# A gated delta-rule layer on one core: z's gates a body later, the heads' sum on ScalarE and GpSimd, weights in three pieces, new engine orders

## The reference

```python
mixed = hidden_states @ w_qkv
z = (hidden_states @ w_z).reshape(Bq, Sq, NUM_V_HEADS, DV)
b, a = hidden_states @ w_b, hidden_states @ w_a
mixed = jax.nn.silu(_causal_conv(mixed, conv_w))          # 4 taps
q, k, v = jnp.split(mixed, [KEY_DIM, 2 * KEY_DIM], axis=-1)
beta = jax.nn.sigmoid(b)
g = -jnp.exp(A_log) * jax.nn.softplus(a + dt_bias)
def step(state, xs):                                      # q, k l2-normalised
    state = state * jnp.exp(g_t)[..., None, None]
    kv = jnp.einsum('bhk,bhkv->bhv', k_t, state)
    delta = (v_t - kv) * b_t[..., None]
    state = state + jnp.einsum('bhk,bhv->bhkv', k_t, delta)
    return state, jnp.einsum('bhk,bhkv->bhv', q_t, state)
o = outs * jax.nn.silu(z)
o = o * jax.lax.rsqrt(jnp.mean(o * o, axis=-1, keepdims=True) + EPS) * norm_gamma
return o.reshape(Bq, Sq, VALUE_DIM) @ w_out               # the sum over the heads
```

## Time and profile before

| | us |
|---|---|
| median of 3 runs | 2320.44 |
| lowest, highest | 2314.27, 2321.96 |
| profiled execution | 2318.31 |
| its span, first to last instruction | 2316.6 |

### The profile page before, as it was taken

How to read it: one execution, slowest core, us unless ns; L and a number is a source line. 1 busy time by engine, 2 the same in 40 slices (tenths; PEclk the granted TensorE clock), 3 DMA queues, 4 the chain that set the end, 5 groups by cost and what they waited for, 6 DMA issues and landing times. The chain is left out here.

```text
span 2316.6 us, 47612 instructions
## 1 busy us (share of the span) xinstructions
PE 2153.8 (93%) x16494; PEld 1561.7 (67%) x16494; DVE 1843.2 (80%) x3303; ACT 1198.6 (52%) x3805; POOL 1224.3 (53%) x1194
## 2 busy tenths in 40 slices
PE   6899999999999999999999999999999999977998
PEld 3667677666777676767777676767676776754665
DVE  4788788888888888888888887888888788853665
ACT  3555555555655555655555565555565555531110
POOL 3555566565666565566655565655566565530100
PEclk8999999999999999999999999999999999989999
DMA  4587777788777778777777777878878878761000
GB/s 138 130 174 165 181 157 165 158 167 183 165 164 167 162 169 183 171 169 162 166 163 169 183 166 163 161 164 172 183 164 161 157 155 172 156 166 37 28 10 19
DMA packets 597341, 349.81 MB, mean 151 GB/s; under 512 B 487664, under 2 KB 558704, under 8 KB 596848
## 3 DMA queue, kind: packets, MB, share of 16 engines
q1 hardware_dynamic: 597104, 346.78, 68.9%
HBM read 159.50 MB, written 69.73 MB: 99 GB/s over the span
## 5 line engine op out<-in xcount | busy, mean ns | idle before, releaser
L1343 DVE SCALAR_TENSOR_TENSOR conv<-bank,cw_all,conv 128x511 f32<-128x511 f32 (+2 forms) x768 | 568.1, 740 | 18.3 <-ACT conv L1235 6.9
L1056 PE MATMUL bank<-xT,w_kh 128*128 128x512 f32 x1024 | 559.6, 630 | 10.6 <-ACT kraw L1264 10.1
L1288 ACT ACTIVATE X<-bank 128x512 f16<-128x512 f32 x384 | 229.8, 598 | 286.0 <-PE bank L1109 285.9
L1369 DVE TENSOR_TENSOR N<-bank,lev 128x512 f16<-128x512 f32 x320 | 218.5, 683 | 151.1 <-PE bank L1099 151.0
L1235 ACT ACTIVATE conv<-bank,cw_all 128x512 f32<-128x512 f32 x256 | 175.9, 687 | 289.5 <-PE bank L1056 289.5
L1184 PE MATMUL bank<-ogT,wo 128*128 128x512 f32 x512 | 268.3, 628 | 24.4 <-DMA ogT<-o_blocks 23.9
L985 POOL TENSOR_SCALAR_AFFINE_SELECT mhiT<-m32T 128x512 f16<-128x512 f32 x128 | 131.2, 1025 | 255.6 <-DVE m32T L1355 255.6
L1075 PE MATMUL bank<-w_kh,xT 128*128 128x256 f32 x1024 | 248.9, 386 | 0.4 <-DVE conv L1343 0.4
L1075 PEld LDWEIGHTS bank<-w_kh,xT 128*128 128x128 f32 x1024 | 189.8, 192 | 54.0 <-DVE conv L1343 23.7
L1099 PEld LDWEIGHTS bank<-X,mhiT 128*128 128x128 f16 x3072 | 139.9, 98 | 122.4 <-issue 110.5
L1387 DVE SCALAR_TENSOR_TENSOR rhs<-bank,sc_all,vals 128x128 f32<-128x128 f32 x384 | 116.0, 344 | 108.2 <-PE bank L1136 108.2
(11 more groups left out here) (178 smaller groups left out, 4851.9 us busy)
## 6 DMA issues: line engine op xcount, KB each, us to landing
egb<-rows SPq DMA_DIRECT2D x64, 512.0 KB, 4.9
v_blocks<-conv SPq DMA_DIRECT2D x64, 512.0 KB, 3.4
ecb<-rows SPq DMA_DIRECT2D x64, 512.0 KB, 5.2
vT<-v_blocks SPq DMA_DIRECT2D x256, 128.0 KB, 3.2
o_blocks<-og SPq DMA_DIRECT2D x64, 512.0 KB, 3.7
ogT<-o_blocks SPq DMA_DIRECT2D x256, 128.0 KB, 4.3
w_kh<-w_heads SPq DMA_DIRECT2D x16, 768.0 KB, 7.4
XT<-X SPq DMA_TRANSPOSE x384, 3.6
```

Of the source, the lines that this page charges most:

```text
L1056: mm = pe.matmul(PB[j % 2][:, :], w[:, k, g * P:(g + 1) * P], xT[:, k, b * SEQ:(b + 1) * SEQ], start=(k == 0), stop=(k == KT - 1))
L1288: act.activation(blocks(X[:, p], i, 0), packed(IB[p], i), ACT.Copy).then_inc(s_x[p], 1)
L1343: dve.scalar_tensor_tensor(conv[:, g, m:], PB[j % 2][:, 0:SEQ - m], cw_all[:, head, g * TAPS + 3 - m:g * TAPS + 4 - m], conv[:, g, m:], op ...
L1369: dve.tensor_tensor(N[:, p].rearrange("p x (b s) -> p x b s", s=LEVELS[i]), packed(IB[p], i), blocks(lev[:, 1 + i:2 + i, :], i, 0).broadca ...
```

## The change

**z's gates.** `gate` 0 and 1 are done for body k+2 in round k, and `gate` 2 and 3 for body k+1 in the next round's beginning (before: all for body k+3). The banks P0 and P1 therefore hold z of another body than before when `proj` comes, and the waits follow:

```diff
-                        if j < 2 and later:
-                            pe.wait_ge(s_zs, 2 * (n - 1) + j + 1)
+                        if j < 2 and n == 1:
+                            pe.wait_ge(s_conv, 3 * (2 + j) + 3)
+                        if j < 2 and n > 1:
+                            pe.wait_ge(s_zs, 2 * (n - 2) + j + 1)
...
                     if c == 0:
-                        pe.wait_ge(s_conv, 12 * n + 3 * (2 + h) + 3)
+                        pe.wait_ge(s_conv, 12 * min(n + 1, BODIES - 1) + 3 * (2 + h) + 3)
+                        if n == BODIES - 1:
+                            pe.wait_ge(s_zs, 2 * (n - 1) + h + 1)
```

```diff
-                elif name == "acc":
-                    dve.wait_ge(s_opp, n * 2 + i + 1)
...
-                    dve.tensor_tensor(a, OB[i][:, :], a, ALU.add).then_inc(s_acc, 1)
...
+                elif name == "ev":
+                    act.wait_ge(s_opp, n * 2 + i + 1)
+                    act.activation(flat(og2)[:, SEQ * i:SEQ * (i + 1)], OB[i][:, :], ACT.Copy).then_inc(s_ev, 1)
...
+                elif name == "add":
+                    b = n % B
+                    pool.wait_ge(s_ev, 2 * n + i + 1)
...
+                    pool.tensor_tensor(a, flat(og2)[:, SEQ * i:SEQ * (i + 1)], a, ALU.add).then_inc(s_acc, 1)
...
                     if c % 2 == 0 and later:
-                        pe.wait_ge(s_acc, 2 * (n - 1) + c // 2 + 1)
+                        pe.wait_ge(s_ev, 2 * (n - 1) + c // 2 + 1)
...
-                        act.wait_ge(s_ost[1 - n % 2], 16 * ((n - 1) // 2 + 1))
+                        act.wait_ge(s_acc, 2 * n)
```

```diff
-            def weights(kh):
-                if kh > 1:
+            def weights(kh, j):
+                third = slice(256 * j, 256 * (j + 1))
+                if j == 0 and kh > 1:
                     sp.wait_ge(s_proj, 4 * B * (kh - 1))
                     sp.wait_ge(s_zp, 2 * B * (kh - 1))
-                sp.dma_start(w_kh[:, kh % 2], w_heads[kh].rearrange("p (t n) -> p t n", t=KT)).then_inc(s_w, 16)
-                if kh > 0:
-                    sp.wait_ge(s_wog, kh)
-                sp.dma_start(wo_raw[:, :, :], w_out[kh]).then_inc(s_wo, 16)
+                sp.dma_start(w_kh[:, kh % 2, :, third],
+                             w_heads[kh].rearrange("p (t n) -> p t n", t=KT)[:, :, third]).then_inc(s_w, 16)
+                if j == 2:
+                    if kh > 0:
+                        sp.wait_ge(s_wog, kh)
+                    sp.dma_start(wo_raw[:, :, :], w_out[kh]).then_inc(s_wo, 16)
...
-                    if n % B == 1 and n // B + 1 < KH:
-                        weights(n // B + 1)
+                    if n % B > 0 and n // B + 1 < KH:
+                        weights(n // B + 1, n % B - 1)
```

**The orders.** All five lists of `ORDER` are new. SP's:

```diff
-        ("ecs", 0, 2), ("weights", 0, 4), ("flip", 1, 2), ("vld", 0, 2), ("ost", 0, 0), ("flip", 2, 2), ("egs", 0, 4),
-        ("old", 0, 0), ("flip", 3, 2), ("flip", 4, 2), ("x0", 0, 3), ("flip", 5, 2), ("flip", 0, 3), ("vst", 0, 3),
+        ("flip", 5, 1), ("flip", 1, 2), ("weights", 0, 3), ("egs", 0, 3), ("ost", 0, 0), ("vst", 0, 2), ("ecs", 0, 4),
+        ("flip", 2, 2), ("old", 0, 0), ("vld", 0, 2), ("flip", 3, 2), ("x0", 0, 3), ("flip", 4, 2), ("flip", 0, 3),
```

More of the change, by code:

```diff
@@ L31 @@
     "tensor": [
[L32 to L40, removed]
+        ("proj", 0, 3), ("newton", 0, 1), ("join", 1, 2), ("newton", 1, 1), ("proj", 1, 3), ("gate", 2, 1),
@@ new lines @@
+        ("gate", 3, 1), ("growx", 1, 2), ("finish", 0, 1), ("finish", 1, 1), ("proj", 2, 3), ("join", 2, 2),
+        ("solve", 0, 1), ("proj", 3, 3), ("write", 0, 1), ("ktp", 0, 3), ("ktp", 1, 3), ("products", 1, 2),
+        ("read", 1, 1), ("growx", 2, 2), ("products", 0, 3), ("solve", 1, 1), ("proj", 4, 3), ("write", 1, 1),
+        ("ktp", 2, 3), ("ktp", 3, 3), ("join", 3, 2), ("proj", 5, 3), ("read", 2, 1), ("growx", 3, 2), ("proj", 6, 3),
+        ("solve", 2, 1), ("proj", 7, 3), ("write", 2, 1), ("join", 4, 2), ("project", 0, 0), ("project", 1, 0),
@@ L41 @@
+        ("project", 2, 0), ("project", 3, 0), ("growx", 4, 2), ("read", 3, 1), ("out", 0, 1), ("out", 1, 1),
+        ("gate", 0, 2), ("gate", 1, 2), ("solve", 3, 1), ("join", 0, 3), ("join", 5, 2), ("out", 2, 1),
+        ("growx", 0, 3), ("growx", 5, 2), ("out", 3, 1),
     ],
     "scalar": [
-        ("zs", 1, 1), ("tap", 0, 2), ("growx", 1, 1), ("u", 0, 0), ("tap", 1, 2), ("silu", 0, 2), ("squares", 0, 2),
-        ("kraw", 0, 2), ("growx", 2, 1), ("u", 1, 0), ("silu", 1, 2), ("tap", 2, 2), ("squares", 1, 2), ("u", 2, 0),
@@ L45 @@
-        ("growx", 3, 1), ("tap", 3, 2), ("growx", 4, 1), ("vals", 0, 1), ("vals", 1, 1), ("silu", 2, 2),
-        ("join", 5, 1), ("u", 3, 0), ("silu", 3, 2), ("growx", 5, 1), ("growx", 0, 2), ("power", 0, 0), ("zs", 0, 2),
-        ("power", 1, 0),
+        ("power", 1, 0), ("tap", 0, 3), ("zs", 1, 1), ("growx", 1, 2), ("u", 0, 1), ("silu", 0, 3), ("tap", 1, 3),
+        ("squares", 0, 3), ("kraw", 0, 3), ("growx", 2, 2), ("u", 1, 1), ("silu", 1, 3), ("squares", 1, 3),
+        ("growx", 3, 2), ("u", 2, 1), ("tap", 2, 3), ("ev", 0, 0), ("tap", 3, 3), ("vals", 0, 2), ("vals", 1, 2),
@@ L48 @@
+        ("growx", 4, 2), ("ev", 1, 0), ("silu", 2, 3), ("silu", 3, 3), ("zs", 0, 2), ("join", 5, 2), ("u", 3, 1),
+        ("growx", 0, 3), ("growx", 5, 2), ("power", 0, 1),
     ],
     "vector": [
-        ("join", 1, 2), ("tt", 0, 1), ("tt", 1, 1), ("conv", 0, 3), ("conv", 1, 3), ("conv", 2, 3), ("s", 0, 1),
-        ("join", 2, 2), ("conv", 3, 3), ("rhs", 1, 1), ("ot", 0, 0), ("conv", 4, 3), ("conv", 5, 3), ("p", 0, 2),
-        ("s", 1, 1), ("p", 1, 2), ("join", 3, 2), ("rhs", 2, 1), ("conv", 6, 3), ("conv", 7, 3), ("scan", 0, 3),
@@ L233, in build_kernel @@
         s_opp = sem("s_opp")
+        s_ev = sem("s_ev")
         s_acc = sem("s_acc")
@@ L1215, in _ @@
             for name, i, n in rounds(ORDER["tensor"]):
+                if name == "gate" and n == BODIES - 1:
+                    continue
                 run(name, i, n)
+                if (name, i, n) == ("gate", 3, BODIES - 2):
+                    for j in range(4):
+                        run(name, j, BODIES - 1)
                 if n == 0 and (name, i) == ("proj", 2):
@@ L1318, in _ @@
             for name, i, n in rounds(ORDER["scalar"]):
+                if name == "zs" and n == BODIES - 1:
+                    continue
                 run(name, i, n)
+                if (name, i, n) == ("zs", 1, BODIES - 2):
+                    for j in range(2):
+                        run(name, j, BODIES - 1)
                 if n == 0 and (name, i) == ("tap", 0):
```

25 lines of the change are left out of this document (14 added, 11 removed).

## The result

The changed kernel takes 2484.15 us (median of 4 runs, 2482.26 to 2489.66) against 2319.10 for the kernel before (4 runs): a ratio of 1.0718, with the 95% interval 1.0692 to 1.0744. It is 7% slower, and it lies 59 us above the upper end of the range. The profiled execution took 2489.7 us, its span 2487.9.

A forecast was written before the change was run, and what follows sets the result against it. PE was taken to bound the kernel, so only its waits and clock count. From 2318.3 us: - 107 + 78 + 51 + 20 + 6 + 1 = + 49, that is 2367 us; 8-in-10 range 2240 to 2425.

The forecast's parts named there:

- The sign: Whole kernel: slower by over 0.3%, chance 0.60; within 0.3%, 0.05; faster, 0.35.
- B: Rival at growx3: the DMA backlog drains in time, no wait there; 2218 to 2258 us, chance 0.26.
- C: Rival at growx3: backlog drains in part, 0.2 to 0.8 us wait per body; 2255 to 2317 us, chance 0.13.
- D: Rival at ACT's queue: growx4 1 us late delays flip4 and growx5, 60 us more; about 2427 us, chance 0.07.
- What bounds it: Whole kernel: PE, busy 93% of the span, sets the time; edits count only through its idle time or clock.
- (a): Weights in three later pieces: SP no longer stands before wo_raw, saving 3.34 us x 14 = 47 us.
- (b): New order, PE's small waits for S, kraw, XT and project go: together 60 us saved.
- (c): SP's new order: four loads ahead of flip2 make growx3 wait, 78 us; weights' pieces add 51 us.
- The clock: At the third weights piece, a 3.0 us stall lowers PE's clock: 1.3 us x 15 = 20, bounds 0 and 60.
- (e): Heads' sum from DVE to ACT and POOL: costed at nothing, but about 1 us at the last body's end.
- (d): z's gates a body later: proj 2 waits for ACT's silu, at most 0.1 us a body, 6 in all.

The follow-up runs named there:

- the good one: The SP order of the kernel with ecb behind flip3 (2199.48 us); the same kernel with w_kh in one 768 KB transfer took 2232.53 us.
- ecb behind flip3: Changed kernel with SP's list alone rearranged: v_blocks and egb issued ahead of flip1, ecb behind flip3; 2199.48 us, ratio 0.9473 to the kernel before.
- egb, ecb by ACT: Changed kernel with egb and ecb issued by ACT behind its growx1, ecb for body k+3 instead of k+4; 2303.77 us, ratio 0.9930 to the kernel before.
- only egb ahead: Changed kernel with egb issued ahead of flip1, leaving three 512 KB transfers between the flips; 2388.30 us, ratio 1.0275 to the kernel before.
- spread: Changed kernel with SP's list alone rearranged: v_blocks and egb ahead of flip1, ecb behind flip2; 2379.92 us, ratio 1.0253 to the kernel before.
- the old order, with pieces: Kernel before with w_kh alone changed, to three pieces at the same place of SP's list; 2294.70 us, ratio 0.9868 to the kernel before.
- The new order with the sum on DVE: Kernel with ecb behind flip3, but the heads' sum put back on DVE; 2233.46 us, ratio 0.9634 to the kernel before.

## Why the prediction was wrong

The sign and the mechanism of the loss were right: the queue of four 512 KB transfers between flip1 and flip2 makes growx3 wait in nearly every body (61 waits). Of the other cases B (the backlog drains) and C (in part) fell with the 196 us of waits; the ceiling of 435 GB/s that stands beside B was nowhere near, as the row moved 259. D (ACT's queue) fell too: 196 of the 206.5 us for XT stand before growx3, so growx5 can have 10.5 at most, where D needs 60. Step by step:

- **What bounds it.** Right. PE's idle time and clock account for the differences above, but for the sum's in the new order, which hides in PE's busy time.
- **(a) The weights, -47.** Right in kind, and in size -31.6 in the old order and -33 in the good one. This step took the whole loss away, and left out that the pieces themselves make PE wait, for ogT above all (13.4 us more).
- **(b) PE's small waits, -60.** Right for S, kraw and project: 47 us forecast, 20.5 + 9.1 + 14.9 = 44.5 measured. The other 13 us of XT waits stayed for the most part: 206.5 less 196. In the kernel with ecb behind flip3 they are down to 9.2.
- **(c) The row of transfers, +78 and +51.** This is the first term that was mis-sized, and the step at which the prediction failed: 196 us in place of 129. Its places were right. In the body shown, flip1 was issued 1.3 us after growx1 (1.4 forecast) and took 3.1, and PE needed XT 11.0 us after growx1 (1305.59 - 2.61 - 1291.99) where I had 10.8. What failed is "four loads x 1.7 us". In 60 of the 61 bodies that waited flip2 landed on average 9.1 us after flip1 where there were no weights (17 bodies), 9.5 with one piece (28) and 10.9 with piece and wo_raw (15). My steps say 7.65, 8.5 and 9.35. The waits were 2.5, 3.0 and 4.4 us, against 1.3, 2.15 and 3.0. The weights' share was about right (0.4 and 1.8 us between the landings, against 0.85 and 1.7); the row of four with its flip takes longer: 9.1 us for 4 x 512 + 256 KB is 2.0 us for 512 KB and 259 GB/s, below even the lower of the two rates that I had the earlier trace rows. Where there were no weights, the last of the four had landed 7.7 us after flip1, not 6.8, and flip2 1.35 us behind it, not 0.85: two thirds of the miss are the loads, one third is the flip, which I had priced by its bytes. I had taken the spacing of one pair of landings, and the rate of the 3.5 us under them, as the pace of the whole row. Why a long row moves less than a pair no run here shows.
- **The clock, +20.** The second term that was mis-sized, in the main a consequence of the first. I let only the third piece's stall be long enough to lower the clock. As the waits were 0.9 to 1.4 us longer, it came about in each of the three bodies with weights in the windows above, and the longest stall cost twice as much (32.16 - 29.57 = 2.6 us, not 1.3). By the forecast PE's busy time would have been 2153.8 - 14 x 1.3 + 20 = 2156; it was 2208.9, 53 us more. With the 67 us of waits in (c) that is 120 of the 123 us by which the profiled execution missed 2367. The 53 flatters the term: the kernel that differs by SP's list alone, with ecb behind flip3, has 2111.2 us of PE, so the row's stalls lengthened the matmuls by 98 us, beyond the bound of 60 as well. What hid the rest is the sum, in (e).
- **(d) The gates.** Right: nothing measurable.
- **(e) The heads' sum at nothing.** Wrong, and by luck in the other direction. I looked at ACT's and POOL's room and at the cover of out. That PE could gain from a less full DVE wasn't asked, since DVE had 4 us to spare in each body. It brings 34 to 40 us. Without it the same forecast would have missed by some 40 us more: the changed kernel with the sum on DVE takes 2524.

The clock's own share was not tried by an experiment that changes it alone, but the kernels with the new order of PE and the sum on ACT and POOL, all with the same 16494 matmuls, can be put in a row by how long PE stood for the transfer that it waited for most:

| kernel | wait, us (times, mean) | PE busy, us | mean granted clock |
|---|---|---|---|
| ecb behind flip3 | XT 9.2 (17, 0.5) | 2111.2 | 0.986 |
| egb, ecb by ACT | XT 108.8 (81, 1.3) | 2129.8 | 0.982 |
| only egb ahead | XT 151.9 (94, 1.6) | 2156.5 | 0.973 |
| spread | ogT 136.6 (61, 2.2) | 2165.2 | 0.969 |
| changed kernel | XT 206.5 (77, 2.7) | 2208.9 | 0.946 |

Beside 81 waits of 1.3 us the matmuls are 19 us longer than in the first row, beside 77 waits of 2.7 us 98 us. The price of a stall grows faster than the stall.

Two things stay open. One is whether a flip is held up by the order within SP's queue or by the bytes on the shared DMA engines; the run with ACT's queue shows the latter at work and doesn't exclude the former. The other is where the 28 us are by which PE's busy time in the old order, with pieces (2139.2), exceeds that of the best kernel (2111.2) at the same mean clock of 0.986. The new order with the sum on DVE has 2145.2, so the sum alone can be worth that much; but in the old order its move to ACT and POOL made PE's busy time longer (2153.8 to 2165.3).
